# Masked pairs: the second split moves ahead of the next pair's inverse roots, their rows are normalised a stage later, and other pairs' statistics move to mid stage

## The chip, the cores and the metric

The kernel runs on one core of a Trainium2 chip. The metric is the device time of one execution in microseconds (us). A core has five engines with instruction queues of their own: TensorE (PE in the profile, PEld for its weight loads), VectorE (DVE), ScalarE (ACT), GpSimd (POOL) and SyncE (SP, which here only issues DMAs). They meet through semaphores: an instruction may raise one when it is done, and an engine may wait until one has reached a value. What stands behind a waiting instruction on the same engine waits too.

## The reference

Two decoder layers, x of 8 sequences of 128 tokens with 128 features (8 x 128 x 128), each block preceded by a layer norm without weights and added to x:

```python
x = x + L0_attn(ln(x))              # gated linear recurrence
x = x + L0_xattn(ln(x), ctx, ctx)   # cross attention, rotary, 16 heads of 8
x = x + L0_ffn(ln(x))               # 16 routed experts and 2 shared
x = x + L1_attn(ln(x))              # long attention, attention within segments, fusion
x = x + L1_xattn(ln(x), ctx, ctx, mask)   # attention with a given mask
x = x + L1_ffn(ln(x))               # 8 experts, top 2

def _layernorm(x, eps=1e-05):
    m, v = mean(x), var(x)
    return (x - m) / sqrt(v + eps)

def _L1_xattn_ref(q, k, v, mask):   # no projections: q is ln(x), k and v are ctx
    scores = einsum('bhqd,bhkd->bhqk', qh, kh) / sqrt(8)
    scores = where(mask == 0, -1e9, scores)
    return einsum('bhqk,bhkd->bhqd', softmax(scores), vh)
```

## The kernel before

The eight sequences are worked on in four pairs; a pair's two sequences are its units s = 0 and 1. The attention blocks are pipelines over pairs of a kind: `cross` (L0_xattn), `long` and `segment` (the two attentions of L1_attn) and `given`, the masked pairs of L1_xattn. `attention_b` (L315) runs the four cross pairs, `attention_de` (L322) runs twelve: L0, S0, L1, S1, L2, S2, L3, S3 and then the masked pairs G0 to G3. In stage t every engine runs its own `stage(r, p, q, nxt, ...)`, where r is the pair that comes in (the t-th), p the pair before it, q the one before that, and nxt the pair after r, given only when it isn't a segment pair (those share their long pair's normalised rows). So in stage 9 r = G1, p = G0, q = S3, nxt = G2; stage 12 has p = G3, q = G2 and neither r nor nxt. Each engine's order within a stage is written out by hand.

A unit's way through the stages: its rows are normalised; q and k are split on GpSimd into a high and a low half-precision part (`split_high` L486 and L487, `split_low` L505 and L506) in "stacks"; TensorE transposes the stacks (`stack_T`, L823 and L825) and ScalarE copies them out (qkT, L634); TensorE makes scores in two halves of eight heads (`scores`, L846, banks sc0 and sc1); VectorE takes the maxima per query (`maxima`, L1374) and writes them into the stack (L1381, L1383), whose q part is transposed again (`stack_maxima`, L880) and copied out (qmT, L638); transposed scores (`scores_T`, also L846) follow, ScalarE's exponential (probs, L619), numerators (L897) and sums (L904), and VectorE's `normalise` (reciprocal L1389, product L1395). For a masked pair two mask passes go ahead of each half of scores (L835 for `scores`, L833 for `scores_T`).

TensorE's order at the start of a stage is: scores(p,0,0), scores_T(q,1,1), stack_T(p,1), then scores_T(q,1,0), scores(p,0,1) and so on to stack_maxima(p,0), sums, scores(p,1,0). scores_T(q,1,0) uses the bank that maxima(p,0,0) has to have read. VectorE's order is maxima(p,0,0), normalise(q,0), maxima(p,0,1), mid-stage work, maxima(p,1,0), normalise(q,1), maxima(p,1,1), and then what prepares the next pair.

A layer norm is spread over two engines. VectorE's `norm_stats` (L1272, L1277) makes mean and variance of a pair; GpSimd's `rsqrt` adds eps (ln_var, L413) and takes the power -1/2 (rstd, L415); VectorE's `norm_apply` writes the rows xn (L1289). For a masked pair VectorE's `masks_given` (L1461 to L1465) also tests whether a row is masked throughout, GpSimd multiplies rstd by that (rstd_any, L525, semaphore e_q), and `inputs_given` (L1472) writes the mask in the form that TensorE adds. Pairs G0 and G2 keep their rows and statistics in slots 2 and 3, all others in 0 and 1.

Two places set the order around the change:

```python
rsqrt((LN_B if nxt.kind == "cross" else LN_D) + nxt.norm, 2, at=at)   # GpSimd, then
split_high(r, 1)
split_low(r, 1)
```

On GpSimd the inverse roots of nxt stand ahead of the second split of r, in every stage that has both; they wait for VectorE's statistics of nxt, which come behind maxima(p,1,1) at the end of the stage. `norm_apply` of nxt then ends VectorE's stage. In the stages with r = G2 and G3 GpSimd also has a weight split (`weights1_low`, w_lo, L449) behind the second split. The second split of a masked pair from G1 on, and that of a cross pair, waits for stack_maxima(p,1) (L880) of the same stage, since that reads the stack that it writes over.

SP's loads of context and mask for the pairs 2 and 3 wait for GpSimd's value copies (`copy_values`, L466) and VectorE's L1461 of the pair two before.

Of the kernel before, what the change touches and what calls it, by code (L numbers as in the profile page):

```python
# [44 lines left out]
ALU = mybir.AluOpType  # L45
# [35 lines left out]
def program(nc, A, out):  # L81
    ctx = ExitStack()
    with ctx:
# [18 lines left out]
        rstd = sb("rstd", [128, B])  # L102
# [179 lines left out]
        def slot_of(p):  # L282

            return 2 if p.kind == "given" and p.i % 2 == 0 else 0
# [122 lines left out]
        def _(pool):  # L407
            def rsqrt(group, count, at=0):

                var = ln_var[:, 0:count]  # L410
                pool.wait_ge(ln_stats, 2 * group + 2)
                pool.sem_inc(wait_held_p, 1)
                pool.tensor_scalar(var, mv[:, at:at + count, 1], EPS, None, ALU.add).then_inc(ln_step, 1)  # L413
                pool.wait_ge(ln_step, LN_STEPS * group + 1)
                pool.tensor_tensor(rstd[:, at:at + count], var, minus_half[:, 0:count], ALU.pow).then_inc(ln_step, 1)  # L415
                pool.wait_ge(ln_step, LN_STEPS * group + 2)
# [82 lines left out]
            def split_low(r, s):  # L499
                q_all, k_all, _ = stacks_of(r)  # L500
                qq, kk, _ = parts(r, s)
                qs = q_all[:, s, :].rearrange("p (h c) -> p h c", c=SLOT)
                ks = k_all[:, s, :].rearrange("p (h c) -> p h c", c=SLOT)
                pool.wait_ge(u_hi, r.n + s + 1)
                pool.tensor_tensor(qs[:, :, 16:24], heads(qq), qs[:, :, 0:8], ALU.subtract)  # L505
                pool.tensor_tensor(ks[:, :, 8:16], heads(kk), ks[:, :, 0:8], ALU.subtract).then_inc(u_lo, 1)  # L506

            def stage(r, p, q, nxt=None, late=None, ahead=None, last=None):
                if p:
                    copy_values(p, 0)  # L510
                if r:
                    if r.kind == "segment":
                        segment_rows(r)
                    split_high(r, 0)
                    split_low(r, 0)
                if p:
                    copy_values(p, 1)
                if ahead:
                    rsqrt(ahead, 4, at=4)
                if nxt:  # L520
                    at = slot_of(nxt)
                    rsqrt((LN_B if nxt.kind == "cross" else LN_D) + nxt.norm, 2, at=at)
                    if nxt.kind == "given":
                        pool.wait_ge(e_any, 3 * nxt.i + 3)
                        pool.tensor_tensor(rstd_any[:, at:at + 2], rstd[:, at:at + 2], mask_any[:, :, 1], ALU.mult)\  # L525
                            .then_inc(e_q, 1)
                if r:
                    split_high(r, 1)
                    split_low(r, 1)
                if r and r.kind == "cross" and r.i:  # L530
                    weights_low(r.i - 1, r.i - 1)
                if r and r.kind == "given" and r.i >= 2:
                    weights1_low(r.i - 2, r.i - 2)
# [733 lines left out]
        def _(dve):  # L1267
# [344 lines left out]
            def stage(r, p, q, nxt=None, late=None, ahead=None, last=None):  # L1612
                if p:
                    maxima(p, 0, 0)
                if q:
                    normalise(q, 0)
                if p:
                    maxima(p, 0, 1)
                if r and r.kind == "cross":
                    rotate(r, 0)  # L1620
                if r and r.kind == "cross" and not p:
                    add_read(1)
                    dve.wait_ge(x_done, 2)
                if r and r.kind == "segment":
                    counts(r)
                if ahead:
                    if ahead == LN_C:
                        dve.wait_ge(x_done, 4)
                    else:
                        dve.wait_ge(x_end, 2)  # L1630
                    norm_stats(0, 4, ahead, at=4)
                if last:
                    low_part(last, 0)
                    clamp(last, 0)
                if last == LN_F:
                    route1_scores(0)

                if p:
                    maxima(p, 1, 0)
                if late:  # L1640
                    outputs(late)
                if last == LN_C:
                    route_scores(0)
                if q:
                    normalise(q, 1)
                if last == LN_C:
                    route_pairs(0)
                if last == LN_F:
                    route1_weights(0)
                if p:  # L1650
                    maxima(p, 1, 1)
                if ahead:
                    norm_apply(0, 4, ahead, at=4)
                if nxt:
                    if nxt.kind == "given":
                        masks_after = r if r and r.kind == "given" else None
                        if masks_after:
                            inputs_given(masks_after)
                        masks_given(nxt)
                        dve.wait_ge(x_done, OUT_D + nxt.i + 1)  # L1660
                    norm_stats(2 * nxt.i, 2, (LN_B if nxt.kind == "cross" else LN_D) + nxt.norm, at=slot_of(nxt))
                elif r and r.kind == "given":
                    inputs_given(r)
                if r and r.kind == "cross":
                    rotate(r, 1)
                if r and r.kind == "long":
                    inputs_segment(segment(r.i))
                if q and q.kind == "segment":
                    short_rows(q)
                if r and r.kind == "segment":  # L1670
                    if q:
                        dve.wait_ge(d_short, q.i + 1)
                    alone(r)
                if nxt:
                    at, scale = slot_of(nxt), rstd
                    if nxt.kind == "given":
                        dve.wait_ge(e_q, nxt.i + 1)
                        scale = rstd_any
                    if r and r.kind == "segment":
                        dve.wait_ge(d_lx, 9 * r.i + 9)  # L1680
                    norm_apply(2 * nxt.i, 2, (LN_B if nxt.kind == "cross" else LN_D) + nxt.norm, at=at, scale=scale)
                if q and q.kind in ("cross", "given"):
                    outputs(q)
                if last:
                    if last == LN_C:
                        dve.wait_ge(x_done, 5)
                    else:
                        dve.wait_ge(x_end, 3)
                    early_stats(4, 2)
# [194 lines left out]
```

## Time and profile before

| | |
|---|---|
| median of 3 runs | 498.4 us (497.85 to 498.58) |
| the profiled execution, its own time | 498.25 us |
| its span, first to last instruction | 496.4 us |
| PE busy | 426.7 us (86% of the span) |
| DVE busy | 363.7 us (73%) |
| ACT busy | 270.3 us (54%) |
| POOL busy | 163.8 us (33%) |
| mean granted TensorE clock | 0.962 |

All times in the rows are microseconds from the start of the span, for one execution taken by the profiler. A row of a timeline merges neighbouring instructions of one line; in brackets is the idle time of its engine just before, and what ended it. Busy TensorE is not TensorE at its peak, since matmuls are pipelined and their ends are modelled. The granted clock is 1.00 at 2.4 GHz and 0.50 at 1.2 GHz; a mean over a stretch lies between.

### The profile page before, as it was taken

Reading aid. Unit: us, or ns where it says so; the run is one execution under the profiler, and the core shown is the slowest. Engines: PE = TensorE matmul, PEld = TensorE weight load, DVE = VectorE, ACT = ScalarE, POOL = GpSimd, SP = SyncE. Lnnn points to the kernel's source line nnn. Section 1 sums busy time; section 2 is a strip of 40 time slices with the busy share of each in tenths; the row PEclk is TensorE's granted clock in tenths of the full one; section 3 lists DMA queues with packets and bytes.
Section 4 is the critical chain, followed back from the end, with each engine's and each line's share of the span. In section 5 each row is a group of like instructions: output and inputs, shape, how many; then the busy total and the mean of one; then the engine's idle time right before and its main releaser. Section 6 shows DMA issues by size and latency. Waiting matters only on the chain.

```text
span 496.4 us, 14119 instructions
## 1 busy us (share of the span) xinstructions
PE 426.7 (86%) x5646; PEld 278.9 (56%) x5646; DVE 363.7 (73%) x906; ACT 270.3 (54%) x399; POOL 163.8 (33%) x297
## 2 busy tenths in 40 slices
PE   1898788889769999878888887698798999999996
PEld 0555456555336666456565655555454647776775
DVE  5475567778798888557868688655656783999995
ACT  1411455552647767256666565343444576777862
POOL 7003234212358886443323333213224011121110
PEclk9999799998999999979999999879979989999999
DMA  7000000000011132000000000000000001112101
GB/s 260 7 1 12 12 18 18 19 2 1 16 34 49 48 98 77 2 1 3 3 2 3 3 1 3 1 24 2 23 3 1 1 2 44 44 54 76 42 1 44
DMA packets 9066, 13.10 MB, mean 26 GB/s; under 512 B 1450, under 2 KB 7474, under 8 KB 9010
## 3 DMA queue, kind: packets, MB, share of 16 engines
q1 hardware_dynamic: 9012, 12.32, 8.0%
q8 instruction: 41, 0.67, 0.6%
q14 instruction: 13, 0.11, 0.1%
HBM read 11.79 MB, written 0.52 MB: 25 GB/s over the span
## 4 chain that ended last, share of the span: by engine, by line
PE 58%; DVE 24%; POOL 6%; ACT 6%; issue 4%; DMA 1%; DVEq 0%; POOLq 0%; ACTq 0%
DVE smax L1374 8%; PE bk L904 5%; PE sc L846 4%; PE bk L897 3%; PE bk L1227 3%; PE bk L1217 3%; PE bk L1219 3%; PE sc L1077 3%; PE sc L1078 3%; PE sc L1079 3%; DVE inv_sum L1389 2%; PE bk L948 2%; PE bk L880 2%; POOL rstd L415 2%; PE sc L833 2%
## 5 line engine op out<-in xcount | busy, mean ns | idle before, releaser
L1374 DVE TENSOR_REDUCE smax<-sc 128x8 f32<-128x1024 f32 x64 | 78.1, 1220 | 62.3 <-PE sc L846 62.0
L619 ACT ACTIVATE probs<-sc 128x1024 f32<-128x1024 f32 x64 | 65.1, 1025 | 62.8 <-PE sc L846 62.7
L1707 DVE SCALAR_TENSOR_TENSOR x_all<-bk,comb,x_all 128x128 f32<-128x128 f32 x192 | 53.7, 344 | 1.4 <-PE bk L1227 1.3
L541 POOL TENSOR_TENSOR gated_lo<-gated,gated_hi 128x512 f16<-128x512 f32 x36 | 41.7, 1160 | 28.8 <-ACT gated_hi L700 27.5
L735 ACT ACTIVATE probs<-sc,w 128x512 f32<-128x512 f32 x64 | 41.1, 687 | 16.6 <-PE sc L1079 16.5
L897 PE MATMUL bk<-probs,v_pad 128*32 128x128 f32 x1024 | 39.1, 298 | 3.7 <-issue 2.4
L413 POOL TENSOR_SCALAR ln_var<-mv 128x2 f32<-128x2 f32 (+1 forms) x18 | 4.5, 250 | 110.3 <-DVE mv L1277 110.1
L1785 DVE TENSOR_TENSOR p_lo<-probs,p_hi 128x1024 f16<-128x1024 f32 x32 | 38.4, 1223 | 3.4 <-ACT p_hi L742 2.8
L449 POOL TENSOR_TENSOR w_lo<-w,w_hi 128x1024 f16<-128x1024 f32 x8 | 18.0, 2248 | 61.6 <-ACT w_hi L615 61.6
L904 PE MATMUL bk<-probs,ones_pad 128*32 128x128 f32 x1024 | 37.2, 290 | 0.0
L634 ACT ACTIVATE qkT<-bk 128x1024 f16<-128x1024 f16 x32 | 32.6, 1020 | 7.9 <-PE bk L825 7.9
L638 ACT ACTIVATE qmT<-bk 128x512 f16<-128x512 f16 x32 | 19.1, 597 | 32.4 <-PE bk L880 32.4
L700 ACT ACTIVATE gated_hi<-gated 128x512 f16<-128x512 f32 x36 | 22.7, 631 | 25.0 <-DVE gated L1719 24.9
L846 PE MATMUL sc<-qmT,qkT 32*128 32x128 f16 x512 | 25.4, 219 | 11.9 <-DVE smax L1374 11.0
L897 PEld LDWEIGHTS bk<-probs,v_pad 128*32 128x32 f32 x1024 | 29.1, 118 | 11.0 <-issue 9.1
L1176 PE MATMUL bk<-w_hi,gated_hi 128*128 128x128 f16 x144 | 26.4, 221 | 9.8 <-issue 3.8
L1389 DVE RECIPROCAL inv_sum<-bk 128x128 f32<-128x128 f32 x32 | 30.4, 949 | 1.8 <-PE bk L904 1.8
L904 PEld LDWEIGHTS bk<-probs,ones_pad 128*32 128x32 f32 x1024 | 28.4, 117 | 4.0 <-issue 1.0
L1217 PE MATMUL bk<-w_hi,p_hi 128*128 128x128 f16 x256 | 30.3, 219 | 0.0
L1219 PE MATMUL bk<-w_lo,p_hi 128*128 128x128 f16 x256 | 30.3, 219 | 0.0
L846 PEld LDWEIGHTS sc<-qmT,qkT 32*128 32x128 f16 x512 | 14.9, 93 | 23.5 <-issue 22.3
L846 PE MATMUL sc<-qkT 24*128 24x128 f16 (+1 forms) x512 | 26.0, 220 | 1.3 <-ACT probs L619 1.3
(254 smaller groups left out, 1071.1 us busy)
## 6 DMA issues: line engine op xcount, KB each, us to landing
w<-in_w SPq DMA_DIRECT2D x8, 514.0 KB, 3.5
w<-in_w SPq DMA_DIRECT2D x18, 192.0 KB, 2.3
wd<-in_wd SPq DMA_DIRECT2D x1, 644.0 KB
x_all<-in_x SPq DMA_DIRECT2D x1, 512.0 KB, 4.1
ctxT<-in_ctx_t SPq DMA_DIRECT2D x4, 128.0 KB, 3.3
ctx_tok<-in_ctx SPq DMA_DIRECT2D x4, 128.0 KB, 2.2
mask_in<-in_mask SPq DMA_DIRECT2D x4, 128.0 KB, 2.5
out<-x_all SPq DMA_DIRECT2D x1, 512.0 KB, 3.2
```

Of the source, the lines that this page charges most:

```text
L541: pool.tensor_tensor(gated_lo[:, k % DEPTH, :], gated[:, k % DEPTH, :], gated_hi[:, k % DEPTH, :], ALU.subtract).then_inc(c_glo, 1)
L619: act.activation(probs[:, n % 2, half, :], sc[half][:, :], ACT.Exp, scale=HD ** -0.5).then_inc(u_exp, 1)
L735: act.activation(hid[:, k % 2, fc, :], (bank_a, bank_b, bank_c, bank_d)[fc], ACT.Gelu, bias=w1[:, k // 2, 1024 + fc:1025 + fc]).then_inc(f ...
L846: mm = pe.matmul(sc[half][:, jj * 512 + g * 128:jj * 512 + (g + 1) * 128], stationary(r, g), moving(r, g), start=not mask, stop=True, skip ...
L897: pe.matmul(AV[32 * g:32 * g + 32, :], v_pad[:, s, g, 32 * i:32 * i + 32], probs[:, s, i // 2, c], start=i == J - 1, stop=i == 0)
L904: mm = pe.matmul(SUMS[32 * g:32 * g + 32, :], ones_pad[:, 32 * i:32 * i + 32], probs[:, s, i // 2, c], start=i == J - 1, stop=i == 0)
L1217: pe.matmul(dst, hid_hi[:, h, fc, t], w1_hi[:, slot, c], start=b == 0 and fc == 0, stop=False, skip_group_check=True)
L1219: pe.matmul(dst, hid_hi[:, h, fc, t], w1_lo[:, slot, c], start=False, stop=False, skip_group_check=True)
L1374: dve.tensor_reduce(smax[:, s, 8 * half:8 * half + 8], sc[half][:, :].rearrange("p (h k) -> p h k", k=S), X, ALU.max).then_inc(u_max, 1)
L1389: dve.reciprocal(inv_sum[:, s, :], SUMS).then_inc(u_rsum, 1)
L1707: op = dve.scalar_tensor_tensor(x_all[:, bb, :], (bk4, bk5)[k % 2][:, b * 128:(b + 1) * 128], w, x_all[:, bb, :], ALU.mult, ALU.add)
L1785: dve.tensor_tensor(hid_lo[:, k % 2, fc, :], hid[:, k % 2, fc, :], hid_hi[:, k % 2, fc, :], ALU.subtract).then_inc(f_lo, 1)
```

## The change

On GpSimd, for a masked nxt, the roots and rstd_any move behind split_high(r,1) and split_low(r,1); for other kinds they stay where they are. On VectorE, norm_apply of a masked pair moves from the end of the stage before its own into its own stage, between normalise(q,0) and maxima(p,0,1); it waits there for e_q. norm_stats of cross and long pairs moves from behind maxima(p,1,1) to mid stage, ahead of maxima(p,1,0); that of masked pairs stays. The order of inputs_given(r) and masks_given(nxt) is the same as before.

```diff
--- before.py
+++ after.py
@@ -517,16 +517,17 @@
                     copy_values(p, 1)
                 if ahead:
                     rsqrt(ahead, 4, at=4)
-                if nxt:
-                    at = slot_of(nxt)
-                    rsqrt((LN_B if nxt.kind == "cross" else LN_D) + nxt.norm, 2, at=at)
-                    if nxt.kind == "given":
-                        pool.wait_ge(e_any, 3 * nxt.i + 3)
-                        pool.tensor_tensor(rstd_any[:, at:at + 2], rstd[:, at:at + 2], mask_any[:, :, 1], ALU.mult)\
-                            .then_inc(e_q, 1)
+                if nxt and nxt.kind != "given":
+                    rsqrt((LN_B if nxt.kind == "cross" else LN_D) + nxt.norm, 2)
                 if r:
                     split_high(r, 1)
                     split_low(r, 1)
+                if nxt and nxt.kind == "given":
+                    at = slot_of(nxt)
+                    rsqrt(LN_D + nxt.norm, 2, at=at)
+                    pool.wait_ge(e_any, 3 * nxt.i + 3)
+                    pool.tensor_tensor(rstd_any[:, at:at + 2], rstd[:, at:at + 2], mask_any[:, :, 1], ALU.mult)\
+                        .then_inc(e_q, 1)
                 if r and r.kind == "cross" and r.i:
                     weights_low(r.i - 1, r.i - 1)
                 if r and r.kind == "given" and r.i >= 2:
@@ -1614,6 +1615,9 @@
                     maxima(p, 0, 0)
                 if q:
                     normalise(q, 0)
+                if r and r.kind == "given":
+                    dve.wait_ge(e_q, r.i + 1)
+                    norm_apply(2 * r.i, 2, LN_D + r.norm, at=slot_of(r), scale=rstd_any)
                 if p:
                     maxima(p, 0, 1)
                 if r and r.kind == "cross":
@@ -1623,6 +1627,8 @@
                     dve.wait_ge(x_done, 2)
                 if r and r.kind == "segment":
                     counts(r)
+                if nxt and nxt.kind != "given":
+                    norm_stats(2 * nxt.i, 2, (LN_B if nxt.kind == "cross" else LN_D) + nxt.norm)
                 if ahead:
                     if ahead == LN_C:
                         dve.wait_ge(x_done, 4)
@@ -1651,16 +1657,12 @@
                     maxima(p, 1, 1)
                 if ahead:
                     norm_apply(0, 4, ahead, at=4)
-                if nxt:
-                    if nxt.kind == "given":
-                        masks_after = r if r and r.kind == "given" else None
-                        if masks_after:
-                            inputs_given(masks_after)
-                        masks_given(nxt)
-                        dve.wait_ge(x_done, OUT_D + nxt.i + 1)
-                    norm_stats(2 * nxt.i, 2, (LN_B if nxt.kind == "cross" else LN_D) + nxt.norm, at=slot_of(nxt))
-                elif r and r.kind == "given":
+                if r and r.kind == "given":
                     inputs_given(r)
+                if nxt and nxt.kind == "given":
+                    masks_given(nxt)
+                    dve.wait_ge(x_done, OUT_D + nxt.i + 1)
+                    norm_stats(2 * nxt.i, 2, LN_D + nxt.norm, at=slot_of(nxt))
                 if r and r.kind == "cross":
                     rotate(r, 1)
                 if r and r.kind == "long":
@@ -1671,14 +1673,10 @@
                     if q:
                         dve.wait_ge(d_short, q.i + 1)
                     alone(r)
-                if nxt:
-                    at, scale = slot_of(nxt), rstd
-                    if nxt.kind == "given":
-                        dve.wait_ge(e_q, nxt.i + 1)
-                        scale = rstd_any
+                if nxt and nxt.kind != "given":
                     if r and r.kind == "segment":
                         dve.wait_ge(d_lx, 9 * r.i + 9)
-                    norm_apply(2 * nxt.i, 2, (LN_B if nxt.kind == "cross" else LN_D) + nxt.norm, at=at, scale=scale)
+                    norm_apply(2 * nxt.i, 2, (LN_B if nxt.kind == "cross" else LN_D) + nxt.norm)
                 if q and q.kind in ("cross", "given"):
                     outputs(q)
                 if last:
```

## Rows read from the trace of the kernel before

**Rows 1.** The chain that ended last, by engine (part 4 of the page)

```profile
PE 58%; DVE 24%; POOL 6%; ACT 6%; issue 4%; DMA 1%; DVEq 0%; POOLq 0%; ACTq 0%
```

**Rows 2.** TensorE's timeline: start us, us, engine, operation [idle before <-releaser]

```profile
319.43 0.60 PE L835 MATMUL sc<-mask_b,ident_b 128*128 128x512 bf16 x2
...
322.48 0.61 PE L823 MATMUL bk<-ident_h,q_stack 128*128 128x128 f16 x4 [2.10 <-POOL k_stack L506]
...
340.80 0.40 PE L823 MATMUL bk<-ident_h,q_stack 128*128 128x128 f16 x4 [1.28 <-POOL k_stack L506]
...
353.88 0.40 PE L880 MATMUL bk<-ident_h,q_stack 128*128 128x128 f16 x4 [0.44 <-DVE q_stack L1383]
...
355.22 0.60 PE L835 MATMUL sc<-mask_b,ident_b 128*128 128x512 bf16 x2
...
359.28 0.40 PE L823 MATMUL bk<-ident_h,q_stack 128*128 128x128 f16 x4 [2.26 <-POOL k_stack L506]
...
374.35 0.60 PE L835 MATMUL sc<-mask_b,ident_b 128*128 128x512 bf16 x2
```

**Rows 3.** GpSimd's timeline at the end of stage 10 (same columns)

```profile
356.32 0.22 POOL L413 TENSOR_SCALAR ln_var<-mv 128x2 f32<-128x2 f32 x1 [8.79 <-DVE mv L1277]
...
357.58 0.40 POOL L486 CAST q_stack<-xn 128x256 f16<-128x256 f32 x1
...
359.18 2.12 POOL L449 TENSOR_TENSOR w_lo<-w,w_hi 128x1024 f16<-128x1024 f32 x1
```

**Rows 4.** VectorE's timeline, stages 9 to 12 (same columns)

```profile
330.50 1.23 DVE L1374 TENSOR_REDUCE smax<-sc 128x8 f32<-128x1024 f32 x1 [3.17 <-PE sc L846]
...
355.25 0.49 DVE L1272 BATCH_NORM_STATS2 stats<-x_all 128x6 f32<-128x128 f32 x2
...
357.67 0.73 DVE L1289 TENSOR_SCALAR xn<-x_all,mv,rstd_any 128x128 f32<-128x128 f32 x2 [1.54 <-POOL rstd_any L525]
358.32 0.41 DVE L1483 TENSOR_TENSOR x_all<-bk,x_all 128x256 f32<-128x256 f32 x1
...
368.03 1.23 DVE L1374 TENSOR_REDUCE smax<-sc 128x8 f32<-128x1024 f32 x1 [3.19 <-PE sc L846]
...
375.33 1.23 DVE L1374 TENSOR_REDUCE smax<-sc 128x8 f32<-128x1024 f32 x1 [1.69 <-PE sc L846]
...
378.53 1.23 DVE L1374 TENSOR_REDUCE smax<-sc 128x8 f32<-128x1024 f32 x1 [0.71 <-PE sc L846]
...
382.63 1.23 DVE L1374 TENSOR_REDUCE smax<-sc 128x8 f32<-128x1024 f32 x1 [1.09 <-PE sc L846]
```

**Rows 5.** Stretches: us, busy of PE, PEld, DVE, ACT, POOL, granted clock, DMA

```profile
315.50:318.90 3.40, 3.34 (x56) 2.72 (x60) 3.16 (x10) 1.55 (x3) 0.00 (x0) 0.50 0.02 5
...
322.30:329.10 6.80, 6.62 (x86) 4.41 (x90) 3.26 (x6) 2.54 (x3) 1.23 (x5) 0.50 0.01 2
...
359.90:366.70 6.80, 6.69 (x80) 3.86 (x84) 2.78 (x5) 2.54 (x3) 2.59 (x5) 0.50 0.01 2
366.70:396.00 29.30, 27.59 (x468) 15.90 (x457) 19.88 (x55) 15.07 (x18) 6.32 (x12) 1.00 0.01 2
```

**Rows 6.** Timelines of VectorE, ScalarE and TensorE, stages 5 and 6

```profile
269.48 1.23 DVE L1374 TENSOR_REDUCE smax<-sc 128x8 f32<-128x1024 f32 x1 [1.58 <-PE sc L846]
...
274.42 0.61 DVE L1491 SCALAR_TENSOR_TENSOR short<-bk,lone,lone_x 128x128 f32<-128x128 f32 x2
...
280.69 0.23 DVE L1383 SCALAR_TENSOR_TENSOR q_seg<-smax,q_seg 128x16 f16<-128x16 f32 x1
...
273.91 0.47 ACT L672 ACTIVATE longT<-bk,lt_bo 128x256 f32<-128x256 f32 x1 [0.30 <-PE bk L1016]
...
281.21 0.38 PE L880 MATMUL bk<-ident_h,q_seg 128*128 128x128 f16 x4 [0.29 <-ACT qkT L634]
```

**Rows 7.** GpSimd's timeline, the second split of cross stage 2

```profile
77.45 0.40 POOL L486 CAST q_stack<-qkv 128x256 f16<-128x256 f32 x1 [0.27 <-PE bk L880]
```

**Rows 8.** One line's instructions: normalised rows with rstd_any (min/median/max ns)

```profile
L1289 DVE TENSOR_SCALAR xn<-x_all,mv,rstd_any x8: 383/405/427, 304.2 to 358.0; 128x128 f32<-128x128 f32 x8
```

## The prediction

> **What bounds the kernel now.** I read the chain of work that ended last first: TensorE carries 58% of the span, VectorE 24%, GpSimd only 6% [rows 1]. An average says little about one stretch, so I went to TensorE's timeline of the masked stages and looked, in each, for the row after the opening scores: the transposes of the second split (L823). In stages 9, 10 and 11 TensorE stands idle before it for 2.10, 1.28 and 2.26 us, each time until GpSimd's last split instruction (L506) [rows 2]; stage 8 has a stall of this kind too. Stage 12, which no further pair follows, has the same opening without it: it is my template.
>
> Next, GpSimd's timeline ahead of one stall (end of stage 10): ln_var starts at 356.32 after waiting 8.79 us for the statistics, the split's first cast follows at 357.58, and at 359.18 GpSimd is through with it and starts on w_lo [rows 3]; TensorE goes on at 359.28 [rows 2]. So the roots (1.26 us) and the split (1.60) stand one behind the other, and the split, whose own inputs were there, waits for statistics that VectorE makes last in its stage. VectorE loses too: it waits 1.54 us for rstd_any before xn, and the next maximum is queued behind that [rows 4].
>
> The stalls have a second price. In 322.3:329.1 and 359.9:366.7 the granted clock is 0.50, the 1.2 GHz level, each time right behind a stall over 2 us; in 315.5:318.9 it is 0.50 without one [rows 2, 5]. TensorE is busy 6.62 and 6.69 of the 6.80 us there [rows 5], so its work is stretched.
>
> **Part 1: split ahead of the roots, rows normalised in the next stage (stages 7 to 11).** No instruction is added or removed. Four split instructions on GpSimd move past three of the roots and their waits; two xn instructions move past a maximum and a reciprocal with its product. No DMA moves: SP's loads of the later pairs wait for GpSimd's value copies and VectorE's mask test, which keep their places and shift with the stages. w_lo (2.12 us [rows 3]) stays behind the roots.
>
> I compare the length from a stage's first score pass to its third maximum. Stage 12: 374.35 to 382.63 = 8.28 us [rows 2, 4]. In it VectorE idles 0.71 us before the second maximum [rows 4], just where xn will stand; an xn pair takes 0.73. So xn costs about nothing in stages 10 and 11, which have stage 12's mask passes; in stage 9 q is a segment pair, its transposed scores have none, TensorE is sooner, and I count xn whole.
> - Stage 9: 319.43 to 330.50 = 11.07 now [rows 2, 4]; then 8.28 - 0.71 + 0.73 = 8.30. Gain 2.8.
> - Stage 10 has the late fusion in this length, so I go by its stall. In stage 11 the stall begins at 359.28 - 2.26 = 357.02, 1.80 after the start; in stage 10 at 340.80 - 1.28 = 339.52, so it starts at 337.72 [rows 2]. By stage 12 the first maximum begins 0.98 later (374.35 to 375.33) and lasts 1.23 [rows 2, 4]: sc0 is free at 339.93, when TensorE still has the split's transposes to do. Little takes the stall's place: 1.2 of 1.28.
> - Stage 11: 355.22 to 368.03 = 12.81 now [rows 2, 4]. VectorE is through with statistics at 357.67 - 1.54 = 356.13 and then has the output addition (L1483, 0.41) [rows 4], so the first maximum starts at 356.54 and not at 355.22 + 0.98 = 356.20, 0.34 late. Then 8.62. Gain 4.2.
>
> Sum 8.2. Of it 4.7 is idle time: 1.2 in stage 10, and in stages 9 and 11 the stall less the wait for the first maximum that is left. In stage 9 the transposes would start at 322.48 - 2.10 = 320.38, take about 0.6, and the maximum ends at 319.43 + 0.98 + 1.23 = 321.64: 0.7 left, 1.4 gained; in stage 11 the same sum with 357.02 and 357.77 leaves 0.2 and gains 2.1. The other 3.5 is work at 2.4 GHz instead of 1.2, as stage 12 shows it.
>
> What is late next? A masked pair's second split waits for the last transposes of its stage (L880), at 353.88 + 0.40 = 354.28 [rows 2], 0.94 before the next stage. Split 1.60 and roots 1.26 then put rstd_any some 2.0 us into that stage. VectorE comes to xn after 0.98 + 1.23 + 1.26, the last for reciprocal and product (376.56 to 378.53 - 0.71 in stage 12 [rows 4]), at 3.5. So the new wait, with the stage's other maxima queued behind it, has 1.5 us to spare. The first split of the next pair needs xn, but also the stage's first maxima transposes, which come later still.
>
> Stage 8: the stall goes, but VectorE binds: it runs there from maximum to maximum without a gap, and xn, gone before the first, comes back before the second. Gain as in part 2, 0.35.
>
> **Part 2: statistics of cross and long pairs in mid stage.** Six places. Their cover is VectorE's idle time before the third maximum, 1.58 us in stage 5 [rows 6]; this repeats in stage 3 and, a little longer, in two cross stages. Without the cover each would cost its own length, 356.13 - 355.25 = 0.88 us by stage 10's [rows 4], which I keep for the range for the first stages, where the gap is shorter. In stages 3 and 5 the split's stall goes. But short (L1491) starts at 274.42, right at the end of ACT's longT (273.91 + 0.47) [rows 6], so VectorE enters the next stage no sooner. The next transposes there (L880) wait now until 281.21 behind ACT's qkT; then VectorE's q_seg write will bind, at 280.69 + 0.23 + 0.05 = 280.97 [rows 6]. Gain 0.24; the same pair of rows gives 0.45 in stage 4 and 0.35 in stage 8. Cross stages: the second split starts behind L880, after 0.27 us idle, and not behind the roots [rows 7]: 0.
>
> **Sum.** 2.8 + 1.2 + 4.2 + 0.35 + 0.24 + 0.45 = 9.2 us. The profiled execution took 498.25 us, 1.85 over its span of 496.4 and 0.15 under the median of 498.4. Taken off the median: 489.2 us.
>
> **Bounds of what the old trace does not show.** xn ahead of the second maximum: 0 to 0.73 in each of four stages. The clock: with both half-speed stretches back, part 1 gives 4.7 and not 8.2; if the one at 315.5 goes too, up to half of its 3.34 busy us comes on top, of which I take 1.0, since VectorE's statistics end soon behind. I take the middle: the template ran at 1.00 [rows 5] with such short waits as will be left.
>
> **Contention.** The split will run beside VectorE's statistics, and w_lo beside xn of stage 11. The row: xn in the rstd_any form, which each time starts together with the split's casts, takes 383 to 427 ns (eight of them [rows 3, 4, 8]), a spread of 44 ns; that is in the 0.73. The Trainium skill (SBUF — State Buffer, Who interferes with whom) says that GpSimd and some VectorE forms share a port pair as an exclusive lock, the loser waiting out the whole instruction. By that rule a cast would hold xn back by most of its 0.40 us; the trace does not agree for this pair of forms. Rival 3 gives the sum by the rule.
>
> **Rivals.**
> 1. The clock falls again in stage 9 or 11, since waits of 0.5 to 1.2 us stay. For it: the stretch at 315.5 fell without a stall over 2 us. Against: the template. Both back: 489.2 + 3.5 = 492.7; one: about 491.0. Chance 0.21.
> 2. The stretch at 315.5 runs at 2.4 GHz too: 488.2. Chance 0.10.
> 3. Locking: in stage 11 w_lo would run from about 357.6 to 359.7 (roots from 356.3, then 2.12) and hold xn, due at 356.54 + 1.23 + 1.26 = 359.0, by 0.7; a cast (0.40) would hold the mask test: 490.3. Chance 0.04.
> 4. A wait takes the stall's place everywhere as it does in stages 3 and 5, where VectorE lets little through. If 30% of 2.10 + 1.28 + 2.26 is gained, that is 1.7, with 1.0 from the rest: 495.7, or within 1 us of no change if the rest fails. For it: the first maximum gates the next scores. Against: stage 12. Chance 0.06.
> 5. Slower: xn waits for rstd_any in mid stage with the maxima behind it. It decides from 1.5 us beyond my reckoning; every us past that is lost in stages 9, 10 and 11. Roots 5 us late: 3 x 3.5 = 10.5 against 9.2, so 499.7. Against: they hang on nothing but the split and statistics of the stage before. Chance 0.04.
>
> **Numbers.** Forecast 0.55. A measurement of this kernel tells about 0.2%, 1 us, from no change. Faster takes the forecast, rivals 1 to 3 and a third of 4: 0.92; same 0.04; slower 0.04. The range 487.2 to 492.7 holds the forecast, both clock rivals and the bounds of xn, and leaves out rivals 4 and 5.
>
> **What would show it.** Right: no idle over 1 us before L823 in stages 8 to 11; stage 9 near 8.3, stage 11 near 8.6; clock 1.00 from stage 9 on; no idle before xn; L880 in stages 4, 6 and 8 released by q_seg. Wrong: xn waiting for rstd_any, clock 0.50 in stage 9 or 11, statistics pushing a third maximum.

## The result, and the profile after

The changed kernel takes 490.84 us, the median of four executions (488.93 to 491.86), beside 498.49 for the kernel before: ratio 0.984, 95% interval 0.982 to 0.9859. By the ratio that is 8.0 us less (7.0 to 9.0; the two medians are 7.65 apart), where 9.2 were forecast; the time lies inside the range of 487.2 to 492.7. The profiled execution took 490.37 us with a span of 488.6; the profiled one of before 498.25 with 496.4, so these two are 7.9 us apart and serve well for the question where the time went.

The chain that ended last, by engine (part 4 of the page), answers to [rows 1]. GpSimd's share has halved, and TensorE and VectorE have taken it over:

```profile
PE 61%; DVE 26%; ACT 5%; issue 4%; POOL 3%; DMA 1%; DVEq 0%; POOLq 0%; ACTq 0%
```

TensorE's timeline of stages 8 to 11 (start us, us, engine, operation [idle before <-releaser]) answers to [rows 2]; lines stand one higher than before, L824 was L823 and L881 was L880:

```profile
303.27 0.23 PE L847 MATMUL sc<-qkT 30*128 30x128 f16 x2
...
305.07 0.34 PE L847 MATMUL sc<-qmT,qkT 32*128 32x128 f16 x6 [0.61 <-DVE smax L1375]
...
306.30 1.08 PE L898 MATMUL bk<-probs,v_pad 128*32 128x128 f32 x32 [0.68 <-DVE aoT L1396]
308.60 0.40 PE L881 MATMUL bk<-ident_h,q_seg 128*128 128x128 f16 x4 [1.23 <-DVE q_seg L1384]
308.93 1.91 PE L905 MATMUL bk<-probs,ones_pad 128*32 128x128 f32 x32
...
313.01 0.23 PE L847 MATMUL sc<-qkT 30*128 30x128 f16 x2
...
319.95 0.61 PE L836 MATMUL sc<-mask_b,ident_b 128*128 128x512 bf16 x2
...
320.85 0.40 PE L824 MATMUL bk<-ident_h,q_stack 128*128 128x128 f16 x4
...
325.62 0.40 PE L881 MATMUL bk<-ident_h,q_stack 128*128 128x128 f16 x4 [1.02 <-DVE q_stack L1384]
...
335.16 0.61 PE L836 MATMUL sc<-mask_b,ident_b 128*128 128x512 bf16 x2
...
336.89 0.40 PE L824 MATMUL bk<-ident_h,q_stack 128*128 128x128 f16 x4
...
351.31 0.60 PE L836 MATMUL sc<-mask_b,ident_b 128*128 128x512 bf16 x2
...
353.05 0.40 PE L824 MATMUL bk<-ident_h,q_stack 128*128 128x128 f16 x4
...
357.84 0.40 PE L881 MATMUL bk<-ident_h,q_stack 128*128 128x128 f16 x4 [1.24 <-DVE q_stack L1384]
```

None of the rows at L824 has an idle time in brackets any more: the three stalls of 2.10, 1.28 and 2.26 us are gone, and so is stage 8's. What TensorE waits for longest now is VectorE, at the transposes of the maxima (L881). GpSimd's timeline at the end of stage 10 shows why the stalls are gone, beside [rows 3]: the split's first cast is there first, and the roots come behind it, with a wait of 0.23 us for the statistics instead of 8.79:

```profile
350.54 0.40 POOL L486 CAST q_stack<-xn 128x256 f16<-128x256 f32 x1 [6.91 <-PE bk L881]
...
352.42 0.22 POOL L413 TENSOR_SCALAR ln_var<-mv 128x2 f32<-128x2 f32 x1 [0.23 <-DVE mv L1278]
...
353.53 0.20 POOL L529 TENSOR_TENSOR rstd_any<-rstd,mask_any 128x2 f32<-128x2 f32 x1
353.68 2.13 POOL L449 TENSOR_TENSOR w_lo<-w,w_hi 128x1024 f16<-128x1024 f32 x1
```

On VectorE's timeline the normalised rows (L1290) never wait for rstd_any. In stages 8 to 10 a pair takes 0.59 or 0.60 us; in stage 11 it takes 1.31, while w_lo above runs until 355.81:

```profile
323.34 0.60 DVE L1290 TENSOR_SCALAR xn<-x_all,mv,rstd_any 128x128 f32<-128x128 f32 x2
...
327.94 1.23 DVE L1375 TENSOR_REDUCE smax<-sc 128x8 f32<-128x1024 f32 x1 [2.37 <-PE sc L847]
...
345.00 1.23 DVE L1375 TENSOR_REDUCE smax<-sc 128x8 f32<-128x1024 f32 x1 [3.87 <-PE sc L847]
...
354.84 1.31 DVE L1290 TENSOR_SCALAR xn<-x_all,mv,rstd_any 128x128 f32<-128x128 f32 x2
...
360.16 1.23 DVE L1375 TENSOR_REDUCE smax<-sc 128x8 f32<-128x1024 f32 x1 [2.37 <-PE sc L847]
```

Last the stretches (us, busy of PE, PEld, DVE, ACT, POOL, granted clock, DMA) of stage 8, of two pieces of it, and of all that follows up to 400, beside [rows 5]:

```profile
303.27:319.95 16.68, 12.53 (x232) 9.48 (x229) 11.11 (x26) 7.40 (x9) 4.07 (x12) 0.80 0.01 2
308.85:312.25 3.40, 3.40 (x41) 2.54 (x38) 0.00 (x0) 0.60 (x1) 1.15 (x4) 0.52 0.00 0
315.70:319.10 3.40, 2.80 (x44) 2.24 (x48) 3.12 (x10) 1.78 (x3) 0.00 (x0) 0.52 0.02 5
319.10:400.00 80.90, 73.43 (x1139) 42.41 (x1131) 57.47 (x160) 43.63 (x56) 21.72 (x47) 1.00 0.03 9
```

The two half-speed stretches of stages 9 and 11 are gone; from 319.1 on the clock is at the 2.4 GHz level. But stage 8 has two now, where it had one. By length from the first score pass to the third maximum, stage 9 takes 7.99 us (11.07 before), stage 10 9.84 (11.18), stage 11 8.85 (12.81): 3.08, 1.34 and 3.96, together 8.38 us gained. Stage 8, from its first score pass to that of stage 9, takes 16.68 (15.80 before): 0.88 lost. The kernel before had these rows in stage 8 (TensorE's timeline):

```profile
303.63 0.23 PE L846 MATMUL sc<-qkT 30*128 30x128 f16 x2
...
305.78 0.40 PE L823 MATMUL bk<-ident_h,q_seg 128*128 128x128 f16 x4 [1.73 <-POOL k_seg L506]
...
309.35 0.38 PE L880 MATMUL bk<-ident_h,q_seg 128*128 128x128 f16 x4 [0.64 <-ACT qkT L634]
309.67 1.08 PE L904 MATMUL bk<-probs,ones_pad 128*32 128x128 f32 x32
...
312.28 0.23 PE L846 MATMUL sc<-qkT 30*128 30x128 f16 x2
```

The clock in this stretch of it was at its full level (columns as in [rows 5]):

```profile
303.00:315.00 12.00, 8.10 (x188) 5.80 (x176) 7.74 (x16) 5.66 (x8) 4.51 (x13) 1.00 0.01 1
```

So up to its first sums (L905, L904 in the kernel before) stage 8 is 0.38 shorter (308.93 - 303.27 = 5.66, before 309.67 - 303.63 = 6.04). The new half-speed stretch behind costs 1.47 (313.01 - 308.93 = 4.08, before 312.28 - 309.67 = 2.61), and the rest, which has a half-speed stretch in both kernels, is 0.21 shorter. Stages 4 and 6 give 0.42 and 0.22; 0.26 was behind before the first of these pairs, 0.17 of it at 46 us, ahead of anything that the change touches. 8.38 - 0.88 + 0.64 - 0.26 = 7.88.

### The profile page after: what moved, and what is told of

It reads as the page before. It is cut to its first block, busy times and chain, and to the rows that moved or that the text cites. A ratio compares the mean times of both kernels' runs of the same rounds, so it can differ in the third digit from the quotient of the medians.

```text
span 488.6 us, 14119 instructions
## 1 busy us (share of the span) xinstructions
PE 422.0 (86%) x5646; PEld 277.1 (57%) x5646; DVE 364.3 (75%) x906; ACT 269.8 (55%) x399; POOL 162.8 (33%) x297
## 4 chain that ended last, share of the span: by engine, by line
PE 61%; DVE 26%; ACT 5%; issue 4%; POOL 3%; DMA 1%; DVEq 0%; POOLq 0%; ACTq 0%
DVE smax L1375 10%; PE bk L905 6%; PE sc L847 4%; PE bk L898 3%; PE bk L1218 3%; PE bk L1228 3%; PE bk L1220 3%; PE sc L1078 3%; PE sc L1079 3%; PE sc L1080 3%; DVE inv_sum L1390 3%; PE bk L881 2%; PE bk L949 2%; DVE xn L1290 2%; DVE gated L1717 2%
## 5 line engine op out<-in xcount | busy, mean ns | idle before, releaser
L898 PE MATMUL bk<-probs,v_pad 128*32 128x128 f32 x1024 | 37.2, 289 | 3.9 <-issue 2.0
L905 PE MATMUL bk<-probs,ones_pad 128*32 128x128 f32 x1024 | 36.8, 287 | 0.0
L898 PEld LDWEIGHTS bk<-probs,v_pad 128*32 128x32 f32 x1024 | 28.1, 115 | 10.5 <-issue 9.0
L486 POOL CAST q_stack<-qkv 128x256 f16<-128x256 f32 x16 | 6.4, 402 | 71.7 <-PE bk L881 31.5
L905 PEld LDWEIGHTS bk<-probs,ones_pad 128*32 128x32 f32 x1024 | 27.9, 115 | 3.6 <-issue 0.6
```

The source lines that it names most:

```text
L898: pe.matmul(AV[32 * g:32 * g + 32, :], v_pad[:, s, g, 32 * i:32 * i + 32], probs[:, s, i // 2, c], start=i == J - 1, stop=i == 0)
L905: mm = pe.matmul(SUMS[32 * g:32 * g + 32, :], ones_pad[:, 32 * i:32 * i + 32], probs[:, s, i // 2, c], start=i == J - 1, stop=i == 0)
```

## The experiments

Ratios are to the kernel before, timed on the same chip beside each (498.7 to 499.1 us there). My theory was that the two moves of the masked half work only together, that half of the gain is clock, and that stage 8's waits for VectorE and w_lo beside the rows of stage 11 gave some of it back.

**1. The masked half alone.** The statistics go back to the end of the stage:

```diff
-                if nxt and nxt.kind != "given":
-                    norm_stats(...)          # mid stage
...
+                if nxt and nxt.kind != "given":
+                    norm_stats(...)          # behind masks_given and its statistics
```

> The changed kernel with the statistics of the other pairs put back to the end of the stage; the masked pairs' half of the change alone. Theory (the masked half gives nearly everything): stages 4 and 6 wait at the first score transposes of the second split as in the kernel before and lose the 0.42 and 0.22 us that the trace of after shows as won there; all else as in after: 490.8 + 0.6 = 491.5 us, 0.986 of before. Rival (the statistics, put between the maxima, lengthen the VectorE chain that TensorE waits for and so cost more than they win, for instance by setting up the half-speed stretch of stage 8): 490 us or less.

Measured: 490.42 us, 0.9837 (0.9822 to 0.9853). The theory's size is not told apart from after's 0.984, but in this trace stages 4 and 6 are as long again as before the change (5.57 and 5.38 us from their second to their third maximum, 5.15 and 5.16 in after), and stage 6 waits for the scalar engine again, as in [rows 6] (TensorE's timeline):

```profile
280.70 0.38 PE L881 MATMUL bk<-ident_h,q_seg 128*128 128x128 f16 x4 [0.29 <-ACT qkT L635]
```

The masked half gives all that a time of the whole kernel can show. The rival (statistics that cost more than they win, and set up the half-speed stretches of stage 8) has no support: stage 8 has such stretches here as well and takes 321.08 - 303.12 = 17.96 us by its first score passes.

**2. The statistics alone.**

```diff
+                if nxt and nxt.kind != "given":
+                    norm_stats(...)          # mid stage, ahead of maxima(p, 1, 0)
...
-                    norm_stats(... nxt of any kind ...)
+                        norm_stats(... masked nxt only ...)
```

> The kernel before with the statistics of cross and long pairs moved to mid stage and nothing else; the other half of the change alone. Theory: stages 4 and 6 gain 0.42 and 0.22 us, the stalls of stages 9, 10 and 11 (2.10, 1.28 and 2.26 us ended by GpSimd's k_stack) and the half-speed stretches behind them stay: 498.5 - 0.6 = 497.9 us, 0.9987. Rival 1 (the second split is late for another reason): 498.5. Rival 2 (the statistics push the maxima, 0.16 us and more per stage): 499 or more.

Measured: 499.06 us, 0.9993 (0.9976 to 1.001). This holds 0.9987 and no change alike. In the trace stages 4 and 6 gain 0.42 and 0.22 us by their third maxima, as in after. So this half is worth 0.6 us by the trace, which is below what a time can show. Rival 2's 499 lies in the interval too; against it stand these two stages.

**3 and 4. Each move of the masked half alone.** First GpSimd's new order with the rows at their old place, at the end of the stage before:

```diff
-                if r and r.kind == "given":
-                    dve.wait_ge(e_q, r.i + 1)
-                    norm_apply(2 * r.i, 2, LN_D + r.norm, at=slot_of(r), scale=rstd_any)
...
+                if nxt and nxt.kind == "given":
+                    dve.wait_ge(e_q, nxt.i + 1)
+                    norm_apply(2 * nxt.i, 2, LN_D + nxt.norm, at=slot_of(nxt), scale=rstd_any)
```

> The changed kernel with the normalised rows of a masked pair back at the end of the stage before, GpSimd's new order kept (second split first, then the roots). Theory (the order alone does not help, as VectorE then waits at the end of the stage for roots that come behind the split): the roots end at 337.3 us in stage 10 of after, the first maximum there would come behind them and the rows, near 337.9 instead of 336.1 us; 1.2 to 1.8 us more at each of the four starts of a stage with a masked pair: 496 to 498 us. Rival (the order is all there is to it): 490.8 us.

Measured: 499.24 us, 1.0006 (0.9989 to 1.0022): the whole gain is gone, somewhat more than expected. The stall has changed its releaser. TensorE's timeline of this kernel, at the scores that need the first maximum of stages 9, 10 and 11:

```profile
322.67 0.40 PE L847 MATMUL sc<-qmT,qkT 32*128 32x128 f16 x8 [2.75 <-DVE smax L1375]
...
339.34 0.59 PE L834 MATMUL sc<-ident_b,mask_b 128*128 128x512 bf16 x2 [1.47 <-DVE smax L1375]
...
359.52 1.01 PE L834 MATMUL sc<-ident_b,mask_b 128*128 128x512 bf16 x2 [4.08 <-DVE smax L1375]
```

And VectorE's, which waits for the roots that now come behind the split; in stage 11 the rows also meet w_lo (355.45, 2.12 us) and take 2.38:

```profile
337.46 0.60 DVE L1290 TENSOR_SCALAR xn<-x_all,mv,rstd_any 128x128 f32<-128x128 f32 x2 [1.73 <-POOL rstd_any L529]
...
355.53 2.38 DVE L1290 TENSOR_SCALAR xn<-x_all,mv,rstd_any 128x128 f32<-128x128 f32 x2 [1.54 <-POOL rstd_any L529]
358.16 1.21 DVE L1375 TENSOR_REDUCE smax<-sc 128x8 f32<-128x1024 f32 x1
```

Then the rows in the next stage with GpSimd's old order:

```diff
-                if nxt and nxt.kind != "given":
-                    rsqrt(...)
+                if nxt:
+                    rsqrt(...)               # and rstd_any for a masked nxt
                 if r:
                     split_high(r, 1)
                     split_low(r, 1)
-                if nxt and nxt.kind == "given":
-                    ...
```

> The changed kernel with GpSimd's old order (the roots of the next masked pair ahead of the second split of this one), the normalised rows kept in the next stage. Theory (the split waits behind roots that wait for statistics at the end of the stage, as before): the stalls of about 2 us at the first score transposes of the second split are back, in stages 8 to 11, with the rows' 0.6 us between the maxima on top: 498 to 500 us. Rival (moving the rows is all there is to it): 490.8 us.

Measured: 498.33 us, 0.998 (0.9965 to 0.9994). TensorE's timeline has the old stalls back, to a few tenths:

```profile
323.32 0.40 PE L823 MATMUL bk<-ident_h,q_stack 128*128 128x128 f16 x4 [1.89 <-POOL k_stack L506]
...
340.35 0.40 PE L823 MATMUL bk<-ident_h,q_stack 128*128 128x128 f16 x4 [1.28 <-POOL k_stack L506]
...
358.82 0.61 PE L823 MATMUL bk<-ident_h,q_stack 128*128 128x128 f16 x4 [2.25 <-POOL k_stack L506]
```

So 0 and 1 us alone (the second 0.3 to 1.7), 8 together. One order makes TensorE wait for the split, the other makes VectorE, and TensorE behind it, wait for the roots; only with the rows' deadline put off is there room for both.

**5. How much of it is clock.** The kernel before, its stalls left as they are, with seven throwaway products in each of two. `keep_busy` is a helper that the kernel already has and uses elsewhere: matmuls whose result nobody reads.

```diff
+                if r and r.kind == "given" and r.i in (1, 3):
+                    keep_busy(bk5[:, :], 7)
                 if p:
                     stack_T(p, 1)
```

> The kernel before with seven throwaway TensorE products (128x512, about 0.22 us apart, 1.5 us in sum) in the wait for the second split of stages 9 and 11 (2.10 and 2.26 us), nothing else changed. They do no part of the computation. The stalls stay as long as they are; only TensorE is no longer idle in them. Theory (the prediction's split of the gain: 3.5 of 8.2 us are the half-speed stretches behind these stalls, and these follow from TensorE's idle): granted clock 1.00 in stages 9 and 11, 498.5 - 3.5 = 495.0 us, 0.993. Rival 1 (the clock falls for another reason than the stall): 498.5 us with the stretches in place. Rival 2 (one of the two stretches stays, as its stage's other waits are enough): 496.5 to 497.2 us.

Measured: 493.87 us, 0.9898 (0.988 to 0.9915): 5.1 us (4.2 to 6.0) from work that nobody needs. TensorE's timeline shows the products in stage 9's stall, and the split no earlier than before (322.62; [rows 2] have 322.48):

```profile
320.31 1.69 PE L923 MATMUL bk<-ident_h 128*128 128x512 f16 x7
322.62 0.40 PE L823 MATMUL bk<-ident_h,q_stack 128*128 128x128 f16 x4 [0.62 <-POOL k_stack L506]
```

The stretches of this kernel, from the first score pass to the third maximum of stages 9 and 11, stand at a granted 1.00:

```profile
319.42:328.57 9.15, 7.72 (x134) 4.28 (x131) 4.72 (x9) 3.56 (x4) 4.56 (x13) 1.00 0.01 2
353.30:364.01 10.71, 9.14 (x138) 4.71 (x135) 5.76 (x14) 4.20 (x5) 6.64 (x14) 1.00 0.01 2
```

11.07 - 9.15 = 1.92 and 12.81 - 10.71 = 2.10: 4.0 us are clock, shown with the stalls still in place. Rivals 1 and 2 of this run fall. The two traced executions are 3.8 us apart; where the rest of the 5.1 lies is not shown. Of the 8.38 us that stages 9 to 11 gave, the other 4.4 are left for idle time.

**6. Stage 8's lost time.** The changed kernel with throwaway products in four of its waits:

```diff
+                if r and r.kind == "given" and r.i == 0:
+                    keep_busy(bk5[:, :], 2)     # ahead of numerators(q.n + 1, 1, r)
+                    keep_busy(bk5[:, :], 4)     # ahead of stack_maxima(p, 0, True)
+                    keep_busy(bk5[:, :], 3)     # ahead of scores_T(p, 0, 0, True)
+                    keep_busy(bk5[:, :], 2)     # ahead of numerators(p.n, 0, r)
```

> The changed kernel with throwaway TensorE products (128x512, 2, 4, 3 and 2 of them) in four of stage 8's waits: ahead of the two value products, of the first transposes of the maxima and of the second half's transposed scores. They do no part of the computation. Theory (the idle of stage 8's waits for VectorE is what makes the clock fall there; the half-speed stretches at 308.9 and 315.7 us of after cost about 2.2 us): granted clock 1.00 all through stage 8, first maximum of stage 8 to that of stage 9 15.0 to 15.5 us instead of 17.2, 488.6 us. Rival 1 (the clock falls there whatever TensorE does in these waits): the stretches stay, 490.8 us. Rival 2 (the throwaway products hold up the work behind them): stage 8 longer, 491 to 492 us.

Measured: 488.25 us, 0.9784 (0.9769 to 0.98), 2.8 us under after by the ratios. Its stretch around stage 8:

```profile
303.00:319.00 16.00, 13.89 (x282) 8.86 (x275) 11.73 (x29) 7.68 (x10) 4.56 (x13) 1.00 0.01 2
```

Stage 8 takes 318.07 - 303.58 = 14.49 us by its first score passes, 2.19 less than in after; from first maximum to first maximum, as the expectation has it, it takes 15.03. Rivals 1 and 2 fall. The time that stage 8 lost is clock, and with TensorE busy in the waits the clock did not fall.

The traces of experiments 1 and 8, whose stage 8 has after's order and waits, bear this out and show its limits. In both the clock falls at the same 1.23 us wait. In the second half of the stage it falls again in experiment 1's and not in experiment 8's, where it stays at 1.00 from 315.0 to 319.0 behind waits of 0.83 and 0.94 us; so stage 8 takes 17.96 and 15.99 us. The first fall in experiment 8's trace:

```profile
308.00:312.00 4.00, 4.00 (x45) 2.99 (x42) 0.00 (x0) 0.60 (x1) 1.62 (x5) 0.59 0.00 0
```

**7. The rows behind the second maximum.**

```diff
-                if r and r.kind == "given":
-                    dve.wait_ge(e_q, r.i + 1)
-                    norm_apply(2 * r.i, 2, LN_D + r.norm, at=slot_of(r), scale=rstd_any)
                 if p:
                     maxima(p, 0, 1)
+                if r and r.kind == "given":
+                    dve.wait_ge(e_q, r.i + 1)
+                    norm_apply(2 * r.i, 2, LN_D + r.norm, at=slot_of(r), scale=rstd_any)
```

> The changed kernel with the normalised rows of a masked pair written behind the second maximum of its first stage instead of ahead of it. Theory A (the rows stand on the path that TensorE's transposes of the maxima wait for): their wait for VectorE's q stack, 1.23, 1.02, 0.81 and 1.24 us in stages 8 to 11 of after, shortens by the rows' 0.60 us in stages 8 and 9, by 0.44 in stage 10 (there the scalar engine's copy of the stack comes next) and by about 1.1 in stage 11: 2.8 us in sum, 488.0 us; with the half-speed stretch in the first half of stage 8 gone too, 1.3 more, 486.7 us. Theory B (only the overlap of the rows with GpSimd's low weights in stage 11 costs anything): 490.1 us. Rival (the first split of the masked pair, which needs the rows, comes too late for its own transposes): stages 8 to 11 longer by up to 1 us each, 491 to 494 us.

Measured: 489.14 us, 0.9806 (0.9792 to 0.982): 1.7 us under after, between theories A and B. From the first to the second maximum it saves 0.51 us in stage 8, 0.25 in stage 9, none in stage 10 and 0.43 in stage 11. Theory A overlooked that the second maximum waits for its scores too: without the rows VectorE idles there until TensorE's pass, so in stage 10 the rows cost nothing and in stage 9 less than half of their length. TensorE's timeline, stages 8 and 11:

```profile
308.85 0.40 PE L881 MATMUL bk<-ident_h,q_seg 128*128 128x128 f16 x4 [0.51 <-DVE q_seg L1384]
...
355.23 0.40 PE L881 MATMUL bk<-ident_h,q_stack 128*128 128x128 f16 x4 [0.81 <-DVE q_stack L1384]
```

Stage 8 has no half-speed stretch in this trace and takes 318.00 - 304.24 = 13.76 us: 0.73 under the one with the throwaway products, which is the rows' share, the other 2.19 the clock's. The 0.73 is more than the 0.51 between the maxima: with the rows ahead of the second maximum, the maxima's write into the stack behind it (L1382) takes 0.41 us beside a split instruction of GpSimd's, and here 0.20 (see the last section). The rival (first split too late) did not show.

**8. Low weights later.** w_lo of stages 10 and 11 a stage later each:

```diff
+                if p and p.kind == "given" and p.i == 3:    # behind copy_values(p, 1)
+                    weights1_low(1, 1)
...
-                if r and r.kind == "given" and r.i >= 2:
-                    weights1_low(r.i - 2, r.i - 2)
+                if r and r.kind == "given" and r.i == 3:
+                    weights1_low(0, 0)
```

> The changed kernel with GpSimd's two subtractions of the low weights (128x1024, 2.13 us each) done one stage later each, so that none lies beside the normalised rows of stage 11. Theory (the two engines get in each other's way in SBUF): the pair of rows in stage 11 takes 0.60 us again instead of 1.31, the transposes of the maxima there wait 0.5 instead of 1.24 us, stage 11 is 0.6 to 0.7 us shorter: 490.1 us. Rival (the rows were slow for another reason, or the wait behind them is set by something else): 1.31 us stays, or the time stays at 490.8 us.

Measured: 489.56 us, 0.9848 (0.9815 to 0.988); these executions run from 486.9 to 493.9, so the time decides nothing. The trace does (VectorE's timeline, stage 11):

```profile
353.25 0.59 DVE L1292 TENSOR_SCALAR xn<-x_all,mv,rstd_any 128x128 f32<-128x128 f32 x2
354.05 1.23 DVE L1377 TENSOR_REDUCE smax<-sc 128x8 f32<-128x1024 f32 x1 [0.20 <-PE sc L849]
```

The pair is back at 0.59, and the first maximum of stage 11 is 7.29 us ahead of the third (350.86 to 358.15) instead of 7.71 (352.45 to 360.16): 0.42 us, the same as with the rows later, and not 0.7. The transposes of the maxima there still wait 0.81 us, not 0.5, mainly because VectorE now waits 0.20 for the scores.

**9. Both remedies.** Rows behind the second maximum, with 2, 1, 3 and 2 throwaway products in stage 8.

> The changed kernel with the rows behind the second maximum and throwaway TensorE products (2, 1, 3 and 2) in the same four waits of stage 8. They do no part of the computation. Theory (with the rows later stage 8 sits so near the edge that in some executions a half-speed stretch falls into it, which makes the spread of 487.8 to 489.4 us; the products keep it away): 487.5 us with a spread below 1 us. Rival 1 (the spread comes from other stretches): 489.1 us. Rival 2 (the products hold up the work behind them by more than the clock gives): 490 us.

Measured: 486.73 us (485.8 to 487.56), 0.9749 (0.9732 to 0.9766): 4.5 us faster than after and 12.5 than before, the fastest of all. Stage 8 takes 13.76 us in the profiled execution, just as in experiment 7's, so the products lengthen nothing there. That the time is 2.8 us under experiment 7's by the ratios would fit a stretch that falls into stage 8 in some of those executions, but it isn't shown: neither profiled execution has one, and 0.9 of the 0.95 us between these two stand ahead of the masked stages. The spread, 1.8 us, is wider than the theory had it.

## Why the prediction was right, point by point

- **Stalls.** "The split, whose own inputs were there, waits for statistics" holds: no idle before L824 in stages 8 to 11. Experiments 3 and 4 add what the prediction only implied, that either move alone gives 0 and 1 us.
- **Stage 9**, forecast 8.30, came to 7.99. The step "I count xn whole" was too cautious: xn took 0.60 and not 0.73, which was its length beside GpSimd's casts, and only 0.25 of it was on the path (experiment 7).
- **Stage 10**, 1.2 forecast, 1.34 measured. The template and the start inferred for this stage served.
- **Stage 11**, forecast 8.62, came to 8.85, two errors that partly cancel. The first maximum started 1.14 us after the first pass, not 1.32; against that stood 0.42 from w_lo beside the rows. That is the first half of rival 3, which the prediction gave 0.04: xn was held by 0.71 us, of which 0.42 reached the stage's length. Of its second half, a cast that holds the mask test, 0.10 us is in the trace (L1466 in stage 7, 0.27 us instead of 0.17). The error was in the step "the trace does not agree for this pair of forms". It went by the lengths in [rows 8], 383 to 427 ns; by its start and end each of these rows waited for the cast's end, as the last section shows.
- **Clock.** 3.5 of 8.2 forecast, 4.0 of 8.38 measured (experiment 5). The template's 1.00 came true in stages 9 and 11.
- **Stage 8** is the step that failed. "The stall goes, but VectorE binds" was right: 0.61, 0.68 and 1.23 us of waits for VectorE, 2.5 in sum, replace 1.73 behind GpSimd and some smaller ones. "Gain as in part 2, 0.35" was not: 0.88 lost, 1.2 off, about the whole error of the forecast. The 0.35 itself came, as 0.38 up to the first sums; what the prediction put at nothing is a new half-speed stretch behind them, which cost 1.47, since its bounds on the clock looked in stage 8 only at the stretch at 315.5. Rival 1 had the right mechanism, a clock that falls on waits of 0.5 to 1.2 us, but looked for it in stages 9 and 11 and not in the one stage where the prediction itself let such waits pile up. At 2.4 GHz throughout, stage 8 of the changed kernel takes 14.49 us (experiment 6).
- **The new wait** had 1.5 us to spare by the forecast; in stage 11 rstd_any ends at 353.73 and xn starts at 354.84, 1.1 later. Rival 5 never came near.
- **Part 2**: 0.45 and 0.24 forecast for stages 4 and 6, 0.42 and 0.22 measured, with L881 released by q_seg as said. In stage 1 the statistics push the third maximum by 0.16 us, made good by the fourth.

What stays open: which waits make the clock fall. In the kernel before, stage 8's first half waits 1.73, 0.42 and 0.64 us and stays at 2.4 GHz; in after it waits less, 0.61, 0.68 and 1.23, and falls. So neither the sum nor the longest wait tells, and the stretch in the second half comes in some traces and not in others. The executions' mean clock, 0.963 to 0.970, fits a varying number of stretches, but only one execution of the changed kernel itself has a trace.

## What to carry to other kernels

Where two engines in turn wait at the end of a stage for something that a third makes late, moving one consumer only hands the wait to the other; look for the pair of moves, and test each alone before calling either the cause. Price a TensorE stall twice, as idle time and as half-speed work that may follow it: it followed 2.10 and 2.26 us here, but not the 2.75 us in stage 9 of experiment 3. Try a few throwaway products in the wait before rebuilding the schedule: fourteen of them took 5 us off the kernel before, where the rebuilt schedule took 8. When a change trades one long wait for several short ones, forecast the clock of that stage anew. And read from a trace when an instruction ends beside its neighbour, not only how long it took.

## What the runs showed of the hardware that was not expected

**Neighbours on VectorE and GpSimd.** One line's instructions in the changed kernel (min/median/max ns), to be read beside [rows 8]:

```profile
L1290 DVE TENSOR_SCALAR xn<-x_all,mv,rstd_any x8: 333/340/1054, 306.1 to 355.8; 128x128 f32<-128x128 f32 x8
```

Alone xn takes about 340 ns. Beside w_lo, a GpSimd subtraction of 128x1024, one took 1054 and ended 0.08 us behind w_lo's end (355.81); a pair took 2.38 in experiment 3. Beside GpSimd's casts it took 383 to 427, which looks like a mild slowdown and is the same wait. In the kernel before, the first xn at the end of stage 10 (VectorE's timeline, a window that holds it alone) ends at 358.05, and the cast beside it ([rows 3], 357.58 + 0.40) at 357.98:

```profile
357.67 0.38 DVE L1289 TENSOR_SCALAR xn<-x_all,mv,rstd_any 128x128 f32<-128x128 f32 x1 [1.54 <-POOL rstd_any L525]
```

That is 0.08 us again, and so with the others of [rows 8]. They lost little because the casts are as short as xn and began with it. Beside a long cast the same line is held for long: near the start of the same trace xn took 2.02 us and ended 0.08 behind GpSimd's (GpSimd's and VectorE's timelines):

```profile
9.80 2.04 POOL L433 CAST bias_hi<-bias_in 2x2176 f16<-2x2176 f32 x1 [0.20 <-POOL rstd L415]
9.90 2.02 DVE L1289 TENSOR_SCALAR xn<-x_all,mv,rstd 128x128 f32<-128x128 f32 x1
```

A smaller one stands in stage 8 of the changed kernel: L1382 (128x16) runs from 307.87 to 308.28 beside L506 (307.80 to 308.23) and takes 0.41 us; in experiment 7, with nothing beside it, 0.20. The Trainium skill (SBUF — State Buffer, Who interferes with whom) describes an exclusive port lock that makes the later instruction wait out the whole of the earlier one; the rows beside w_lo and those beside the casts agree with it.

**The clock fell on waits of about 1 us.** In stage 8 of the changed kernel the granted clock goes to its 1.2 GHz level behind idle times of 0.61, 0.68 and 1.23 us between 304.5 and 308.6, no single one long. Eleven products of 0.22 us in the stage's waits kept it at 2.4 GHz (experiment 6), and in the trace of experiment 7, where the last of the three is 0.51 us, it did not fall either. It is no rule for waits of this length: 0.83 and 0.94 us passed at 2.4 GHz in experiment 8's trace.
